# Two quantising pairs on VectorE moved forward in the first stage of a hybrid transformer kernel

## The chip, the cores and the metric

The kernel runs on one core of one Trainium2 chip. The metric is the device time of one execution in microseconds (us). The time before is 2147.03 us, the median of 3 runs (2146.94 to 2148.97).

## The reference, cut to what matters

The program is four layers one after the other on x (2 x 1024 tokens, width 512): a gated linear recurrence, a feed-forward layer, an attention layer, and the feed-forward layer again. The change lies in the first. There, for each block of tokens:

```
proj = layernorm(x) @ w_in.T ; q, k, v, a, g = split(proj, 5)       # 16 heads of 32
q = q * rsqrt(mean(q*q per head) + eps) ; k = tanh(k)
a = clip(sigmoid(a + 2), 0.6, 0.9995) ; u = k * v
prefix = cumprod(a) in chunks of 64 ; acc = cumsum(u / max(prefix, 1e-6))
memory = prefix * (state + acc)
y = sigmoid(g) * (q * memory) + (1 - sigmoid(g)) * v ; x = x + y @ w_out.T
```

The feed-forward layers use ternary weights, which are worked out beside the first layer, since they depend on nothing else:

```
scale = max(mean(|w|) over a group of 64, 1e-8) ; w_hat = clip(round(w / scale), -1, 1) * scale
```

## The kernel before, in words

The first stage fills about the first 406 us. It has 16 steps: four blocks of 512 tokens, and in each four slices c of 128 columns (four heads). Step s projects q, k, v, a and g for its slice. Beside that, each step makes three pieces (128 x 512) of the ternary weights, pieces 3s, 3s+1 and 3s+2. Every engine has its own list of instructions, carried out in the order written; they meet only at semaphores.

TensorE, in step s (L468 to L489): q projection (8 instructions), the group sum of piece 3s (`group`, L440 to L445), k projection, sums of the squares of q (`head_squares`), v projection, group sum 3s+1, in some steps output products or transposes 0 and 1 of a normalised block, a projection, `spread` (transposes of the root that ScalarE made), output products or transposes 2 and 3, g projection, group sum 3s+2. All group sums go to the one PSUM bank 5. So group n waits for `scaled` n, the first of the two quantising instructions of the piece before it.

VectorE, in step s (L754 to L809): `finish(s-1)` (four tensor instructions, L738 to L749: the output of the step before), `normal_rows` where a block is to be normalised (a small reciprocal, and L708 four times), `quantise(3s)` (L727 reads the PSUM bank and frees it, L730 makes the comparison from SBUF), the mean and reciprocal of the head sums (L764, L768), tanh times v (L774), `quantise(3s+1)`, the clip of a (L787, L788), the first scan L791, L793, the product L796 that releases `q_scaled`, the second scan L798, its carry L800, `quantise(3s+2)`, and `normal_stats` in some steps (L691 four times, L694 four times, L696). For a "mid" block `keep_low` (L715) writes the low halves of its transposed rows; for output steps `add_out` (L720) adds to x.

GpSimd (L647 to L664) does four tensor instructions per piece, once its quantising is done. ScalarE (L565 to L604) takes the absolute value and sign of a piece, copies and activates the projections, and makes the root (L586) that `spread` waits for, behind the reciprocal L768. It also loads two activation tables around that root, and copies the transposes (L555).

The tables that say which step does what come out as follows. Norm statistics (`STATS_IN`) stand at the ends of steps 0, 1, 4, 5, 8 and 12. The roots (`ROOT_IN`) come one step later. The rows and transposes (`TURN_IN`) stand in steps 2, 3, 6, 7, 10 and 14. Output products (`OUT_IN`) stand in steps 4, 8 and 12. A step is called free below if it has neither transposes nor output products: 0, 1, 5, 9, 11, 13 and 15.

Of the kernel before, what the change touches and what calls it, by code (L numbers as in the profile page):

```python
# [34 lines left out]
class Steps:  # L35
# [5 lines left out]
    def did(self, ins):  # L41
        ins.then_inc(self.sem, 1)
        self.k += 1
        return ins
# [4 lines left out]
    def settle(self):  # L49

        self.eng.wait_ge(self.sem, self.value())
# [4 lines left out]
NSTEP = NBLK * KT  # L56
NP = 3
# [8 lines left out]
STATS_IN = {at: g for g, (_, _, at) in enumerate(NORMS)}  # L66
ROOT_IN = {at + 1: g for g, (_, _, at) in enumerate(NORMS)}
TURN_IN = {at + 2: g for g, (_, _, at) in enumerate(NORMS)}
OUT_IN = {KT * (i + 1): i for i in range(NBLK - 1)}
# [195 lines left out]
def phase_first(nc, core, x_in, w_inT, w_outT, w_guT, w_pT, wq1, wq2, wk):  # L265

    with ExitStack() as ctx:  # L267
# [47 lines left out]
        def ring(s, j):  # L315
            return bank[(5 * s + j) % 4]
# [14 lines left out]
        def of(g):  # L331
            return NORMS[g][:2] if g < len(NORMS) else ("full", g - len(NORMS))
# [9 lines left out]
        def x_tile(blk, t):  # L342
            return x[:, (blk * TPB + t) * D:(blk * TPB + t + 1) * D]
# [323 lines left out]
        def _(dve):  # L667
# [15 lines left out]
            def normal_stats(g):  # L683
                kind, blk = of(g)
                b = g % 2
                for t in range(TPB):
                    if g == 0:
                        dve.wait_ge(first_loaded[t], 16)
                    elif kind == "in" and t == 0:
                        dve.wait_ge(x_loaded[blk], 16)  # L690
                    did(dve.bn_stats(stats[b][:, 6 * t:6 * t + 6], x_tile(blk, t)))  # L691
                settle()
                for t in range(TPB):
                    did(dve.bn_aggr(mv[b][:, 2 * t:2 * t + 2], stats[b][:, 6 * t:6 * t + 6]))  # L694
                settle()
                did(dve.tensor_scalar(var[b][:, :], mv[b][:, 1:2 * TPB:2], LN_EPS,  # L696
                                      1.0 / (UP * UP) if kind == "mid" else 1.0, ALU.add, ALU.mult))
                settle()
                dve.sem_inc(var_ready, 1)

            def normal_rows(g):
                _, blk = of(g)
                b = g % 2
                dve.wait_ge(root_ready, g + 1)
                did(dve.reciprocal(inv[b][:, :], dev[b][:, :]))
                settle()
                for t in range(TPB):
                    dve.tensor_scalar(row_of(g, t), x_tile(blk, t), mv[b][:, 2 * t:2 * t + 1], inv[b][:, t:t + 1],  # L708
                                      ALU.subtract, ALU.mult).then_inc(rows_ready, 1)

            def keep_low(g, t):
                kind, blk = of(g)
                if kind == "mid":
                    dve.wait_ge(kept, g * TPB + t + 1)
                    dve.tensor_tensor(half(blk, 1, t), turn_bank(g, t), half(blk, 0, t),  # L715
                                      ALU.subtract).then_inc(low_kept, 1)

            def add_out(i, t):
                dve.wait_ge(out_done, i * TPB + t + 1)
                dve.tensor_tensor(x_tile(i, t), x_tile(i, t), out_bank(i, t), ALU.add).then_inc(out_added, 1)  # L720

            def quantise(n):
                b = n % DEPTH
                dve.wait_ge(group_summed, n + 1)
                if n >= DEPTH:
                    dve.wait_ge(made, n - DEPTH + 1)
                dve.tensor_scalar(sc[b], bank[5], 1.0 / GROUP, 1e-8, ALU.mult, ALU.max).then_inc(scaled, 1)  # L727
                dve.wait_ge(scaled, n + 1)

                dve.scalar_tensor_tensor(hit[b], sc[b], 257.0 / 512, wabs[b],  # L730
                                         ALU.mult, ALU.is_lt).then_inc(hits, 1)

            def finish(s):

                i, c = divmod(s, KT)
                vc = v_sb[s % 2]
                dve.wait_ge(q_scaled, s + 1)
                did(dve.tensor_tensor(t1[:, :], prefix[:, :], t2[:, :], ALU.mult))  # L738
                settle()
                did(dve.tensor_tensor(t1[:, :], t1[:, :], vc, ALU.subtract))  # L740
                settle()
                dve.wait_ge(g_kept, s + 1)
                did(dve.tensor_tensor(t1[:, :], t1[:, :], g_sb, ALU.mult))
                settle()
                if i and c == 0:
                    dve.wait_ge(out_done, i * TPB)
                if s < KT:
                    dve.wait_ge(turned, TPB)
                dve.tensor_tensor(yT[:, c * BLK:(c + 1) * BLK], t1[:, :], vc, ALU.add).then_inc(y_ready, 1)  # L749
                dve.wait_ge(y_ready, s + 1)  # L750
# [3 lines left out]
            for s in range(NSTEP):  # L754
                i, c = divmod(s, KT)
                if s:
                    finish(s - 1)
                g = TURN_IN.get(s)
                if g is not None:
                    normal_rows(g)  # L760
                quantise(NP * s)

                dve.wait_ge(sq_summed, s + 1)
                did(dve.tensor_scalar(mean[:, :], bank[4][:, 0:HPQ], 1.0 / HD, RMS_EPS, ALU.mult, ALU.add))  # L764
                settle()
                if s:
                    dve.wait_ge(spread_root, s)
                dve.reciprocal(inv_q[:, :], mean[:, :]).then_inc(inv_ready, 1)  # L768
                if g is not None:
                    dve.wait_ge(turned, g * TPB + 1)  # L770

                dve.wait_ge(tanhed, s + 1)
                dve.wait_ge(v_kept, s + 1)
                did(dve.scalar_tensor_tensor(t1[:, :], ring(s, 1), 1.0 / FLOOR, v_sb[s % 2], ALU.mult, ALU.mult))  # L774
                settle()
                dve.sem_inc(dve_took, 1)
                quantise(NP * s + 1)
                if s in OUT_IN:
                    for t in (0, 1):
                        add_out(OUT_IN[s], t)  # L780
                if g is not None:
                    for t in (0, 1):
                        keep_low(g, t)
                    dve.wait_ge(turned, g * TPB + TPB)

                dve.wait_ge(sigmoided, s + 1)
                did(dve.tensor_scalar(a_first[:, 0:BLK:CH], ring(s, 3)[:, 0:BLK:CH], 0.6, 0.9995, ALU.max, ALU.min))  # L787
                did(dve.tensor_scalar(a_sb[:, :], ring(s, 3), 0.6, 0.9995, ALU.max, ALU.min))  # L788
                settle()
                dve.sem_inc(dve_took, 1)  # L790
                did(dve.tensor_tensor_scan(prefix[:, :], a_sb[:, :], a_first[:, :], 0.0, ALU.mult, ALU.max))  # L791
                settle()
                did(dve.scalar_tensor_tensor(t1[:, :], prefix[:, :], FLOOR, t1[:, :], ALU.min, ALU.mult))  # L793
                settle()
                dve.wait_ge(spread_done, s + 1)
                dve.tensor_tensor(prefix[:, :], bank[4], q_sb[:, :], ALU.mult).then_inc(q_scaled, 1)  # L796
                start = carry[:, c:c + 1] if i % (NBLK // NB) else 0.0
                did(dve.tensor_tensor_scan(t2[:, :], a_sb[:, :], t1[:, :], start, ALU.mult, ALU.add))  # L798
                settle()
                did(dve.tensor_copy(carry[:, c:c + 1], t2[:, BLK - 1:BLK]))  # L800
                if s in OUT_IN:
                    for t in (2, 3):
                        add_out(OUT_IN[s], t)
                if g is not None:
                    for t in (2, 3):
                        keep_low(g, t)
                quantise(NP * s + 2)
                if s in STATS_IN:
                    normal_stats(STATS_IN[s])  # L809
            finish(NSTEP - 1)  # L810

# [1022 lines left out]
```

## Time and profile before

| What | Value |
|---|---|
| median of 3 runs | 2147.03 us |
| the profiled execution's own time | 2146.67 us |
| its span | 2144.8 us |
| mean granted TensorE clock | 0.989 |
| TensorE matmuls busy | 96% of the span |
| VectorE busy | 59% |
| ScalarE busy | 40% |
| GpSimd busy | 41% |

The span goes from the first to the last recorded instruction. The shares are averages over four layers that differ, so a question about the first stage is answered from the rows of its own 406 us. There a step takes 20 to 30 us; a row of the timeline with a bracket says how long its engine stood idle before it and which instruction ended that.

### The profile page before, as it was taken

The numbers are of one execution on the slowest core, as the hardware profiler recorded it, in microseconds if no ns is written. First come the engines' busy times: TensorE is split into PE (matmuls) and PEld (weight loads), VectorE is DVE, ScalarE is ACT, GpSimd is POOL, SyncE is SP. The second block draws the span as 40 slices with busy tenths as digits, with TensorE's granted clock in tenths as the row PEclk, the third lists the DMA queues.
The fourth block names the chain that finished last, engine by engine and source line by source line (L and its number), as shares of the span: only waits on it lengthen the run. The fifth ranks groups of instructions, "written<-read, shape, count | busy, mean of one in ns | idle before, by whom it ended". The sixth has DMA issues, their size and how long they took to land.

```text
span 2144.8 us, 29394 instructions
## 1 busy us (share of the span) xinstructions
PE 2065.8 (96%) x11824; PEld 904.4 (42%) x11824; DVE 1270.5 (59%) x1838; ACT 855.0 (40%) x1304; POOL 888.7 (41%) x457
## 2 busy tenths in 40 slices
PE   7999999999999999999999999999999989999999
PEld 3444444444444444343434344343433333444444
DVE  5868677657755634455555555555556723675634
ACT  4434344334444322344343434343344442443431
POOL 3757585500000001676766565766756681000000
PEclk9999999999999999999999999999999998999999
DMA  7110111300000020000001010000000111000001
GB/s 230 35 34 30 30 35 33 139 0 1 1 1 1 1 61 12 1 16 16 16 11 21 11 21 1 16 16 16 1 11 6 38 52 40 0 1 20 20 1 40
DMA packets 68999, 55.53 MB, mean 26 GB/s; under 512 B 36800, under 2 KB 55232, under 8 KB 68608
## 3 DMA queue, kind: packets, MB, share of 16 engines
q1 hardware_dynamic: 61952, 41.07, 6.6%
q10 hardware_dynamic: 6912, 12.59, 1.9%
q8 instruction: 94, 1.54, 0.3%
q14 instruction: 41, 0.34, 0.1%
HBM read 43.02 MB, written 10.62 MB: 25 GB/s over the span
## 4 chain that ended last, share of the span: by engine, by line
PE 54%; POOL 4%; DVE 3%; ACT 3%; issue 1%; DVEq 0%; POOLq 0%; ACTq 0%
PE psum L116 9%; PE psum L1151 8%; PE psum L1239 8%; PE psum L1269 7%; PE psum L1299 5%; PE psum L140 5%; POOL b_totals L1523 3%; PE psum L1189 3%; PE psum L1245 2%; PE psum L1257 2%; PE psum L1282 2%; PE psum L1197 1%; PE psum L1275 1%; DVE b_maxima L1586 1%; ACT b_probs L1445 1%
## 5 line engine op out<-in xcount | busy, mean ns | idle before, releaser
L1523 POOL TENSOR_TENSOR b_totals<-b_totals,b_probs 128x2048 f32<-128x2048 f32 (+3 forms) x160 | 515.7, 3223 | 324.4 <-ACT b_probs L1445 318.7
L1586 DVE TENSOR_REDUCE b_maxima<-psum 128x2 f32<-128x1024 f32 (+3 forms) x384 | 350.7, 955 | 407.5 <-PE psum L1245 245.2
L1445 ACT ACTIVATE b_probs<-psum 128x1024 f32<-128x1024 f32 (+3 forms) x320 | 228.2, 765 | 269.4 <-PE psum L1282 168.9
L435 PE MATMUL psum<-hT,a_win 128*128 128x512 f32 x640 | 290.8, 597 | 0.8 <-ACT hT L555 0.8
L116 PE MATMUL psum<-hT,b_early 128*128 128x512 f16 x1024 | 229.2, 384 | 5.2 <-DVE b_middle L202 5.2
L116 PE MATMUL psum<-hT,W 128*128 128x512 f16 x1024 | 226.4, 381 | 3.9 <-DVE a_win L202 3.9
L435 PEld LDWEIGHTS psum<-hT,a_win 128*128 128x128 f32 x640 | 119.4, 191 | 129.4 <-issue 128.1
L116 PEld LDWEIGHTS psum<-hT,b_early 128*128 128x128 bf16 x1024 | 100.7, 99 | 132.7 <-issue 12.6
L116 PEld LDWEIGHTS psum<-hT,W 128*128 128x128 bf16 x1024 | 100.5, 98 | 126.4 <-DVE a_win L202 7.6
L1500 POOL MEMSET b_mask<- 128x128 f32 x1 | 0.2, 204 | 356.8 <-POOLq L267 356.8
L1633 DVE RECIPROCAL b_down<-b_down 128x128 f32<-128x128 f32 x128 | 112.0, 918 | 42.7 <-ACT b_down L1423 42.7
L654 POOL TENSOR_TENSOR a_parts<-a_parts 128x512 bf16<-128x512 bf16 x48 | 60.1, 1252 | 132.8 <-DVE a_parts L730 132.8
L1269 PE MATMUL psum<-b_middle 32*128 32x512 f32 (+3 forms) x768 | 105.1, 535 | 5.8 <-ACT b_probs L1445 5.0
L1239 PE MATMUL psum<-b_early 32*128 32x512 f32 (+3 forms) x768 | 105.0, 537 | 5.2 <-ACT b_probs L1445 2.0
L1445 ACT ACTIVATE b_totals<-psum 128x1024 f32<-128x1024 f32 x64 | 62.0, 1021 | 119.4 <-PE psum L1282 64.1
L1239 PE MATMUL psum<-b_middle 32*128 32x512 f32 (+3 forms) x768 | 103.7, 533 | 2.4 <-ACT b_probs L1445 1.5
L202 DVE SCALAR_TENSOR_TENSOR a_win<-psum,a_win 128x512 f32<-128x512 f32 x64 | 44.2, 692 | 99.6 <-ACT a_win L156 98.6
L202 DVE SCALAR_TENSOR_TENSOR b_middle<-psum,lent 128x512 f32<-128x512 f32 x64 | 44.3, 692 | 96.2 <-ACT lent L156 95.7
L1269 PE MATMUL psum<-b_early 32*128 32x512 f32 (+3 forms) x768 | 100.0, 533 | 1.2 <-DVE b_maxima L1586 1.2
L156 ACT ACTIVATE lent<-psum 128x512 f32<-128x512 f32 x64 | 38.2, 597 | 150.9 <-PE psum L116 150.9
L1151 PE MATMUL psum<-hT,b_middle 128*128 128x512 f32 x192 | 97.9, 619 | 0.0
L140 PE MATMUL psum<-b_down,b_probs 128*128 128x512 bf16 x256 | 97.1, 379 | 0.0
(225 smaller groups left out, 3295.7 us busy)
## 6 DMA issues: line engine op xcount, KB each, us to landing
a_parts<-in_w_guT ACTq DMA_DIRECT2D x32, 256.0 KB, 2.8
ternary<-W SPq DMA_DIRECT2D x1, 6144.0 KB, 18.0
a_win<-in_w_inT SPq DMA_DIRECT2D x20, 256.0 KB, 7.3
a_parts<-in_w_pT ACTq DMA_DIRECT2D x16, 256.0 KB, 2.6
b_down<-lam_rows SPq DMA_DIRECT2D x32, 128.0 KB, 2.8
b_early<-ternary SPq DMA_DIRECT2D x8, 512.0 KB, 8.1
out<-x SPq DMA_DIRECT2D x16, 256.0 KB, 2.2
x<-in_x SPq DMA_DIRECT2D x3, 1024.0 KB, 8.0
```

Of the source, the lines that this page charges most:

```text
L116: last = pe.matmul(self.bank[m % 2 * 2 + part], self.gu[:, k * 2 * HID + col:k * 2 * HID + col + P], self.hT[:, at:at + BLK], start=(k + h ...
L140: last = pe.matmul(self.down_bank(j, t), src[:, m * BLK + t * P:m * BLK + (t + 1) * P], self.wd[:, m * D:(m + 1) * D], start=(m + half == ...
L202: dve.scalar_tensor_tensor(self.h[:, m * BLK:(m + 1) * BLK], self.bank[m % 2 * 2 + 1], 1.0 / UP, self.sg[m % 2], ALU.mult, ALU.mult).then_ ...
L435: last = pe.matmul(ring(s, j), win[:, at:at + P], core["hT"][:, (i * KT + k) * BLK:(i * KT + k + 1) * BLK], start=(k == 0), stop=(k == KT ...
L1151: return pe.matmul(to, weights[:, k * P:(k + 1) * P], hT[:, at:at + BLK], start=(k == 0), stop=(k == KT - 1))
L1239: last = pe.matmul(to[j // 2][:, j % 2, 0:width], strip(qT[w][r % 2], j, qt * P, (qt + 1) * P), strip(kT[w][r % 2], j, kc * BLK, hi), star ...
L1269: pe.matmul(to[j // 2][:, j % 2, off:BLK], strip(kT[w][r % 2], j, kt * P, (kt + 1) * P), strip(qT[w][r % 2], j, c * BLK + off, (c + 1) * B ...
L1299: last = pe.matmul(bank[6][HEAD_AT[j] * HD:(HEAD_AT[j] + 1) * HD, off:BLK], v_rows[r // 2 % 2][:, at:at + HD], held(u, s)[:, j, off:BLK], ...
L1445: act.activation(held(u, s)[:, 2 * a:2 * a + 2, off:BLK], pair_banks(("score", u, s, a))[:, :, off:BLK], ACT.Exp, scale=SCALE).then_inc(ex ...
L1523: pool.tensor_tensor(acc, acc, held(u, s)[:, :, off:BLK], ALU.add).then_inc(summed, 1)
L1586: dve.tensor_reduce(maxima[u % 2][:, :].rearrange("p (h q c) -> p h q c", h=HPT, q=QT)[:, 2 * a:2 * a + 2, qt, kc], pair_banks(("row", u, ...
L1633: last = dve.reciprocal(rden[k % 2][:, cols], rden[k % 2][:, cols])
```

## The change: what it does

Only VectorE's order changes. No instruction is added or removed.

```diff
                 if g is not None:
                     normal_rows(g)
-                quantise(NP * s)
+                if s - 1 not in STATS_IN:
+                    quantise(NP * s)
...
                 did(dve.scalar_tensor_tensor(t1[:, :], prefix[:, :], FLOOR, t1[:, :], ALU.min, ALU.mult))
                 settle()
+                busy = s in OUT_IN or g is not None
+                if not busy:
+                    quantise(NP * s + 2)
                 dve.wait_ge(spread_done, s + 1)
                 dve.tensor_tensor(prefix[:, :], bank[4], q_sb[:, :], ALU.mult).then_inc(q_scaled, 1)
...
-                quantise(NP * s + 2)
+                if busy:
+                    quantise(NP * s + 2)
                 if s in STATS_IN:
+                    if s + 1 < NSTEP:
+                        quantise(NP * (s + 1))
                     normal_stats(STATS_IN[s])
```

In the seven free steps `quantise(3s+2)` goes in front of L796 and the second scan. Behind the six steps with statistics, `quantise(3(s+1))` goes from the next step's start (behind `finish` and, in steps 2 and 6, behind the rows) to the end of step s, in front of the statistics. It touches steps 1, 2, 5, 6, 9 and 13.

## Rows read from the trace of the kernel before

**Rows 1.** The page's first part: busy time, share and instructions of each engine.

```profile
PE 2065.8 (96%) x11824; PEld 904.4 (42%) x11824; DVE 1270.5 (59%) x1838; ACT 855.0 (40%) x1304; POOL 888.7 (41%) x457
```

**Rows 2.** TensorE's waits, first 430 us: line, awaited line, us in total, times, longest.

```profile
PE psum L444 <- DVE a_parts L727: 19.1, 15, 3.5
```

**Rows 3.** Timeline, group sums (TensorE L444) of pieces 3, 7, 14 to 19, 30 and 31.

```profile
38.35 0.38 PE L444 MATMUL psum<-a_parts,groupones 128*128 128x512 bf16 x1 [0.89 <-DVE a_parts L727]
...
70.56 0.38 PE L444 MATMUL psum<-a_parts,groupones 128*128 128x512 bf16 x1 [3.50 <-DVE a_parts L727]
...
136.77 0.38 PE L444 MATMUL psum<-a_parts,groupones 128*128 128x512 bf16 x1
140.42 0.38 PE L444 MATMUL psum<-a_parts,groupones 128*128 128x512 bf16 x1
148.40 0.38 PE L444 MATMUL psum<-a_parts,groupones 128*128 128x512 bf16 x1
155.92 0.38 PE L444 MATMUL psum<-a_parts,groupones 128*128 128x512 bf16 x1
160.93 0.38 PE L444 MATMUL psum<-a_parts,groupones 128*128 128x512 bf16 x1 [1.19 <-DVE a_parts L727]
172.06 0.38 PE L444 MATMUL psum<-a_parts,groupones 128*128 128x512 bf16 x1 [3.00 <-DVE a_parts L727]
...
261.54 0.38 PE L444 MATMUL psum<-a_parts,groupones 128*128 128x512 bf16 x1 [1.21 <-DVE a_parts L727]
270.81 0.38 PE L444 MATMUL psum<-a_parts,groupones 128*128 128x512 bf16 x1 [1.14 <-DVE a_parts L727]
```

**Rows 4.** Timeline, VectorE beside GpSimd: `finish` of steps 1 and 4.

```profile
64.17 1.48 POOL L664 TENSOR_TENSOR W<-a_parts 128x512 bf16<-128x512 bf16 x1
64.67 1.52 DVE L740 TENSOR_TENSOR a_t<-a_t,lent 128x512 f32<-128x512 f32 x1
...
142.38 1.15 POOL L664 TENSOR_TENSOR W<-a_parts 128x512 bf16<-128x512 bf16 x1
142.48 1.61 DVE L738 TENSOR_TENSOR a_t<-a_prefix,a_t 128x512 f32<-128x512 f32 x1
144.12 0.69 DVE L740 TENSOR_TENSOR a_t<-a_t,lent 128x512 f32<-128x512 f32 x1
```

**Rows 5.** Timeline, end of step 4 and step 5.

```profile
137.19 0.69 DVE L727 TENSOR_SCALAR a_parts<-psum 128x512 bf16<-128x512 f32 x1 [2.96 <-PE psum L444]
...
149.30 0.69 DVE L774 SCALAR_TENSOR_TENSOR a_t<-psum,lent 128x512 f32<-128x512 f32 x1 [1.21 <-ACT lent L580]
...
150.70 0.61 ACT L586 ACTIVATE a_qq<-a_inv_q 128x512 f32<-128x512 f32 x1
...
153.32 0.17 DVE L787 TENSOR_SCALAR a_a_first<-psum 128x8 f32<-128x8 f32 x1 [1.38 <-ACT psum L594]
```

**Rows 6.** Timeline, second half of step 5.

```profile
156.42 1.46 DVE L793 SCALAR_TENSOR_TENSOR a_t<-a_prefix,a_t 128x512 f32<-128x512 f32 x1
...
160.09 0.69 DVE L727 TENSOR_SCALAR a_parts<-psum 128x512 bf16<-128x512 f32 x1
...
161.59 1.15 POOL L654 TENSOR_TENSOR a_parts<-a_parts 128x512 bf16<-128x512 bf16 x1 [2.69 <-DVE a_parts L730]
```

**Rows 7.** Timeline, step 6, rows, root, transposes and clip.

```profile
169.41 1.00 DVE L708 TENSOR_SCALAR a_t<-x,a_mv,a_inv 128x512 f32<-128x512 f32 x2
...
172.56 0.17 DVE L764 TENSOR_SCALAR a_mean<-psum 128x16 f32<-128x16 f32 x1
...
173.05 0.63 ACT L586 ACTIVATE a_qq<-a_inv_q 128x512 f32<-128x512 f32 x1 [1.76 <-DVE a_inv_q L768]
173.15 3.60 PE L435 MATMUL psum<-hT,a_win 128*128 128x512 f32 x8
...
174.99 1.08 ACT L555 ACTIVATE hT<-psum 128x512 f16<-128x512 f32 x2
...
178.10 0.17 DVE L787 TENSOR_SCALAR a_a_first<-psum 128x8 f32<-128x8 f32 x1 [1.19 <-PE psum L397]
```

**Rows 8.** Stretches: us, busy time by engine, PEclk (granted clock), DMA.

```profile
72.00:74.00 2.00, 2.00 (x3) 0.67 (x2) 1.75 (x3) 1.97 (x4) 1.84 (x3) 0.50 0.00 0
...
170.00:178.00 8.00, 5.93 (x30) 3.98 (x31) 6.59 (x12) 5.49 (x9) 5.04 (x5) 1.00 0.01 2
```

**Rows 9.** Timeline, TensorE's first wait behind step 15.

```profile
406.96 8.38 PE L116 MATMUL psum<-hT,W 128*128 128x512 f16 x32 [3.34 <-DVE a_win L202]
```

## Prediction

> **What bounds the kernel now.** I read the page's engine shares first: TensorE is busy 96% of the span, VectorE 59% [rows 1]. So time is won where TensorE stands idle. The second view is TensorE's waits in the first 430 us, which hold the stage that the change touches. The reader is to see that nearly all of it is one pair of lines: 19.1 us in 15 waits of the group sum L444 for L727, the instruction that frees its PSUM bank [rows 2]. The third view is the timeline at these group sums [rows 3]. Undisturbed, group 3s to group 3s+1 takes 7.98 us (140.42 to 148.40), and the last group of a step to the first of the next 3.65 us (136.77 to 140.42). A wait stretches them: 155.92 to 160.93 is 5.01 us, 1.36 too long, and 160.93 to 172.06 is 11.13, 3.15 too long. The fourth view is VectorE's and GpSimd's timeline beside each other, since the pair that is moved is work of the one and releases the other.
>
> **The change: what could go.** The same measure over the groups that the edits release gives two sums. Third pieces moved ahead of the second scan, in front of groups 3, 6, 18, 30, 36 and 42: 1.05 + 0.30 + 1.36 + 1.37 + 0.34 + 1.37 = 5.79 us. First pieces moved ahead of the statistics, groups 4, 7 and 19: 1.12 + 3.66 + 3.15 = 7.93 us; groups 16, 28 and 40, also released, wait for nothing now. Together 13.7 us, the ceiling. (Groups 3, 7, 18, 19 and 30 stand in rows 3.) The transfers are untouched: SP's and ScalarE's queues keep their order, and ScalarE's loads wait for nothing that moves later.
>
> **Why little of it arrives: VectorE's own chain.** VectorE does as many instructions as before, in another order. Take step 6. It runs without a gap from L787 at 153.32 [rows 5] to L764 at 172.56 and L774 right behind [rows 7]. L764 leads to the reciprocal, ScalarE's root at 173.05, a table load, the copies L555 at 174.99, then VectorE's L715, and only then have transposes 2 and 3 a free bank. The clip L787 at 178.10 had waited only 1.19 us for them. A TensorE that passes group 19 earlier meets this chain again: the first transpose needs the rows L708, ready 0.5 us after 169.41, and these now stand behind 1.4 us more of quantising. With unchanged durations the rows come at 171.3 and 171.8, the a projection starts at 172.6 and not at 173.15, and L764 does not move. The 4.5 us of waits in steps 5 and 6 would give some 0.5 us. Likewise steps 9 to 10 and 13 to 14: VectorE is the later one at group 31 [rows 3], whose L727 has the same work in front of it as before, so the 1.37 us saved at group 30 is waited at group 31.
>
> **What makes it dearer: GpSimd starts in another place.** The clash is seen in [rows 4]. A VectorE instruction with two SBUF inputs takes 0.69 us (L740 at 144.12), but while GpSimd runs it takes 1.5 to 1.6: GpSimd's L664 holds from 142.38 to 143.53, and L738, issued at 142.48, ends at 144.09, 0.69 us after 143.40. L740 at 64.67 and L664 at 64.17 show the alternation: each waits for the other and a pair takes some 1.56 us. So each clash costs VectorE up to 0.85 us. PSUM-fed L727, L774, L796 and the bn_stats do not clash. Now GpSimd gets piece 17 at 161.59 [rows 6] and nothing until L730 of piece 18 near 172.6; in `finish(5)` only L738 clashes. Afterwards piece 17 starts some 1 us earlier and piece 18 follows it without a gap, eight instructions at 1.23 us or more. They cover `finish(5)`.
>
> The Trainium skill, "GPSIMD Engine Reference", section Specifications, says that GpSimd's SBUF interfaces are shared with VectorE and that the contention is with VectorE instructions in a 2-port mode or with two SBUF inputs. Rows 4 agree, with 0.69 against 1.52 us. A reader who counted only the order of semaphores would come out at the 0.5 us gain above; by this rule step 6 comes out later.
>
> **The sum, step by step.** I place each instruction at its row's duration, with the clash rule, and carry the shift.
>
> Steps 4 to 5 (and 8 to 9, 12 to 13). `quantise(15)` must wait for group 15, which ends at 140.80 [rows 3]; `quantise(14)`, whose L727 starts at 137.19, was over at 138.6 [rows 5]. So VectorE stands idle 2.3 us in front of the statistics. Behind it are L696, `finish(4)` and L764, and ScalarE's root waits for them. The statistics end 3.9 us later, with GpSimd's piece 15 beside `finish(4)`: two or three clashes in place of one. L764 goes from 147.6 to about 151.1. L774 had 1.21 us of idle time and L787 1.38, which soak up most of it, but the root goes from 150.70 to 151.6, the spread and the a gate with it: +0.9 us. The three together +2.7. Lower bound 0 (no extra clash: 2.3 us hidden in the 2.6 us of idle time), upper 1.7 each.
>
> Step 6. From L787 at 154.2: L793 ends 158.8, `quantise(17)` 160.3, L796, the scan ends 162.6, `quantise(18)` 164.1, statistics with a late L696 167.6, `finish(5)` with L738, L740 and L743 clashing 173.2, first row 174.0, second 174.4, L764 175.3 in place of 172.56. The a projection starts at 174.9 (173.15 before), ScalarE's root at 175.8, L715 ends 179.6, transposes 180.2 against 178.06. That is +2.1, of which 0.9 is step 5's; own part +1.2. TensorE stands idle from 168.4 to 174.0, 5.2 us and more. In front of group 7 it stood 3.50 us, and the granted clock at 72 to 74 us was 0.50, its 1.2 GHz level, where 3.00 us in front of group 19 left it at 1.00 [rows 3, 8]. At that level eight projection instructions took 5.3 us, not 3.6. So a second such stretch is likely here, partly under the 0.6 us by which the transposes wait for L715: +0.6. Step 6 together +1.8, from -0.5 to +3.
>
> Steps 0 to 2. In step 1 three of four `finish` instructions clash, not one; L764 goes from 47.95 to about 49.9, the root waits for it, spread +0.75. In step 2 L764 comes at about 74.0 in place of 71.05, the second row at 73.2, the a projection at 73.7 against 71.64: +2.0 if the half-clock stretch falls as it does now, +0.6 if it is over before TensorE resumes. I take +1.5; lower bound -1.3 (no extra clash, VectorE's idle time of 0.95 us in step 1 and what follows), upper +3.
>
> Steps 9 to 10 and 13 to 14: GpSimd gets its piece 2.2 us earlier and is done before the rows: -0.2 each. Step 11: -0.3, group 36 no longer waits. Step 15: `quantise(47)` early puts all of GpSimd's piece 47 on `finish(15)`, with L749 at 407.1 against 406.2: +0.9, and TensorE's wait of 3.34 us there grows [rows 9]; bounds 0 and 1.7.
>
> Sum: 1.5 + 2.7 + 1.8 - 0.4 - 0.3 + 0.9 = +6.2 us. Nothing behind the stage takes it up: the next stages begin when this one ends, and TensorE is their bound. The profiled execution took 2146.67 us, its span and 1.9 us around it; 2146.67 + 6.2 = 2152.9. The median lies 0.36 us higher, 2153.2. I forecast 2153.0.
>
> **The rivals.** (1) No clash effect: GpSimd's earlier pieces fit into gaps, VectorE's chain keeps its length. For it: total GpSimd and VectorE work is unchanged, so clashes may only move. Against it: the pieces now lie exactly on `finish`, which has four instructions of two SBUF inputs in a row. Sum of the lower bounds: -1.3 - 0.5 - 0.3 = -2.1, 2144.9 us, no difference that can be told. Chance 0.22.
> (2) Faster: TensorE's waits do end the steps, and freeing the bank early lets it run ahead, with the step's later waits (rows, root) also coming earlier. Its place is groups 4, 7, 19 and the last group of free steps, its price up to 13.7 us, 2133.3 us; it decides once more than 4.3 us of that arrives. For it speaks the wait table, in which L727 is the only large entry; against it the gapless VectorE chain with 1.19 us of room at L787. Half of it would be 2140. Chance 0.10.
> (3) The same mechanism as mine but heavier: a second half-clock stretch at full price and one more clash in each changed step, 8 x 0.85 + 1: some +14 us, 2161. Chance 0.06.
> The forecast has 0.62.
>
> **How the numbers follow.** Differences within 0.2% (4.3 us) can hardly be told from none. Slower by more than that: the forecast's upper part and rival 3, 0.60; within: rival 1 and the forecast's small outcomes, 0.31; faster 0.09. The range reaches from 2145.0, rival 1, to 2158.5.
>
> **What would show it.** Right: the 15 waits for L727 shrink to about 9, those of groups 4, 7 and 19 gone, and new waits of 4 to 6 us of TensorE for L708 in steps 2 and 6. L743 in `finish(5)` at 1.5 us and not 0.69. VectorE idle 2.3 us for group 15. L764 of step 6 later than now by about 2.7 us. Wrong: if L764 in steps 2 and 6 comes no later, or if the a projection of step 6 starts earlier by over 1 us.

## The result and the profile after

The changed kernel takes 2158.78 us, the median of six runs (2154.94 to 2160.71), against 2148.01 for the kernel before (six runs, 2146.94 to 2152.27). The ratio is 1.0046, with a 95% interval of 1.0033 to 1.0058. It is slower by more than the 0.2% that can be told. By the medians that is 10.8 us, by the ratio 9.9. The profiled execution took 2154.94 us, 8.3 us more than that of before, and its page begins:

```profile
span 2153.1 us, 29392 instructions
...
PE 2071.0 (96%) x11824; PEld 906.9 (42%) x11824; DVE 1276.8 (59%) x1838; ACT 855.7 (40%) x1304; POOL 888.5 (41%) x457
```

GpSimd's busy time is that of [rows 1], VectorE's is 6.3 us more with the same 1838 instructions. TensorE's waits in the first 440 us (line, awaited line, us in total, times, longest):

```profile
PE psum L397 <- DVE a_yo L708: 10.3, 1, 10.3
PE psum L397 <- DVE a_t L708: 10.1, 2, 5.9
PE psum L444 <- DVE a_parts L727: 9.4, 6, 2.9
PE psum L116 <- DVE a_win L202: 4.3, 1, 4.3
PE psum L460 <- ACT a_qq L586: 2.0, 1, 2.0
```

Against [rows 2] the waits for L727 have halved. But transposes (L397) now wait 10.1 us for the normalised rows, once 4.2 us in step 2 and once 5.9 in step 6, and the spread (L460) waits 2.0 us for the root. (The first line is the start of the kernel, as before.) The group sums of pieces 14, 17 to 19 and 31, which answer to [rows 3]:

```profile
137.84 0.38 PE L444 MATMUL psum<-a_parts,groupones 128*128 128x512 bf16 x1
...
157.20 0.38 PE L444 MATMUL psum<-a_parts,groupones 128*128 128x512 bf16 x1
160.85 0.38 PE L444 MATMUL psum<-a_parts,groupones 128*128 128x512 bf16 x1
168.82 0.38 PE L444 MATMUL psum<-a_parts,groupones 128*128 128x512 bf16 x1
...
275.14 0.38 PE L444 MATMUL psum<-a_parts,groupones 128*128 128x512 bf16 x1 [2.92 <-DVE a_parts L727]
```

Groups 18 and 19 come at the undisturbed distances, 3.65 and 7.97 us. Group 19 is 3.24 us ahead of the kernel before, and nothing comes of it: TensorE then waits 5.89 us for the rows. Group 31 waits 2.92 us, where it waited 1.14 and group 30 waited 1.21. The timeline of steps 5 and 6 shows why (start, us, engine, line):

```profile
161.41 1.16 POOL L654 TENSOR_TENSOR a_parts<-a_parts 128x512 bf16<-128x512 bf16 x1 [0.63 <-DVE a_parts L730]
...
167.39 1.15 POOL L654 TENSOR_TENSOR a_parts<-a_parts 128x512 bf16<-128x512 bf16 x1
...
168.71 1.60 DVE L738 TENSOR_TENSOR a_t<-a_prefix,a_t 128x512 f32<-128x512 f32 x1
...
170.35 1.52 DVE L740 TENSOR_TENSOR a_t<-a_t,lent 128x512 f32<-128x512 f32 x1
...
171.90 1.52 DVE L743 TENSOR_TENSOR a_t<-a_t,lent 128x512 f32<-128x512 f32 x1
173.46 0.69 DVE L749 TENSOR_TENSOR a_yo<-a_t,lent 128x512 f32<-128x512 f32 x1
...
174.40 1.00 DVE L708 TENSOR_SCALAR a_t<-x,a_mv,a_inv 128x512 f32<-128x512 f32 x2
175.10 1.94 PE L397 MATMUL psum<-ident,a_t 128*128 128x128 f32 x8 [5.89 <-DVE a_t L708]
...
176.23 0.17 DVE L765 TENSOR_SCALAR a_mean<-psum 128x16 f32<-128x16 f32 x1
...
182.49 0.17 DVE L788 TENSOR_SCALAR a_a_first<-psum 128x8 f32<-128x8 f32 x1 [1.91 <-PE psum L397]
```

GpSimd's piece 17 starts at 161.41 and piece 18 follows it at 167.39. Three of the four `finish(5)` instructions clash with it, where one did. Rows, root and clip all move back: the clip from 178.10 [rows 7] to 182.49, while step 5 began only 1.07 us later than before (group 14, 137.84 against 136.77). The same stretch in the table of stretches (PE, PEld, DVE, ACT, POOL busy, granted clock, DMA):

```profile
171.00:179.00 8.00, 3.90 (x12) 2.80 (x13) 7.44 (x13) 2.46 (x5) 1.85 (x3) 0.57 0.01 2
```

The clock of 0.57 is a mean: 6.8 of the eight us are at the 1.2 GHz level, which is called half clock below. Before, 170 to 178 us had 1.00 [rows 8]. Step 1 has a new half-clock stretch too, behind TensorE's wait of 2.0 us for the root. Its g projection of eight instructions, first in the kernel before, then in the changed one:

```profile
51.53 3.60 PE L435 MATMUL psum<-hT,a_win 128*128 128x512 f32 x8
```

```profile
51.73 5.29 PE L435 MATMUL psum<-hT,a_win 128*128 128x512 f32 x8
```

### The profile page after: what moved, and what is told of

Its sections match the earlier page's. It is cut to its first block, busy times and chain, and to the rows that moved or that the text cites. A ratio compares the mean times of both kernels' runs of the same rounds, so it can differ in the third digit from the quotient of the medians.

```text
span 2153.1 us, 29392 instructions
## 1 busy us (share of the span) xinstructions
PE 2071.0 (96%) x11824; PEld 906.9 (42%) x11824; DVE 1276.8 (59%) x1838; ACT 855.7 (40%) x1304; POOL 888.5 (41%) x457
## 4 chain that ended last, share of the span: by engine, by line
PE 53%; POOL 3%; DVE 3%; ACT 3%; issue 1%; DVEq 0%; POOLq 0%; ACTq 0%
PE psum L116 9%; PE psum L1158 8%; PE psum L1246 8%; PE psum L1276 7%; PE psum L1306 5%; PE psum L140 5%; POOL b_totals L1530 3%; PE psum L1196 3%; PE psum L1252 2%; PE psum L1264 2%; PE psum L1289 2%; PE psum L1204 1%; PE psum L1282 1%; DVE b_maxima L1593 1%; ACT b_probs L1452 1%
## 5 line engine op out<-in xcount | busy, mean ns | idle before, releaser
L202 DVE SCALAR_TENSOR_TENSOR a_win<-psum,a_win 128x512 f32<-128x512 f32 x64 | 44.1, 691 | 101.3 <-ACT a_win L156 100.3
L202 DVE SCALAR_TENSOR_TENSOR b_middle<-psum,lent 128x512 f32<-128x512 f32 x64 | 44.2, 691 | 94.8 <-ACT lent L156 94.3
L140 PE MATMUL psum<-W,a_parts 128*128 128x512 bf16 x256 | 97.0, 379 | 0.0
```

What stands on the lines that cost most here:

```text
L140: last = pe.matmul(self.down_bank(j, t), src[:, m * BLK + t * P:m * BLK + (t + 1) * P], self.wd[:, m * D:(m + 1) * D], start=(m + half == ...
L202: dve.scalar_tensor_tensor(self.h[:, m * BLK:(m + 1) * BLK], self.bank[m % 2 * 2 + 1], 1.0 / UP, self.sg[m % 2], ALU.mult, ALU.mult).then_ ...
```

## Where the time went

The shift of the group sums against the kernel before, read at quiet places, in us; behind the stage it is read at L202 of VectorE. The measured column comes from one profiled execution of each kernel:

| Stretch | measured | forecast |
|---|---|---|
| start of the kernel | +0.2 | 0 |
| steps 0 to 3 | +0.9 | +1.5 |
| step 4 to 5 | +0.2 | +0.9 |
| step 6 | +2.4 | +1.8 |
| steps 8 to 10 | +0.5 | +0.7 |
| step 11 | -0.3 | -0.3 |
| steps 12 to 14 | +2.8 | +0.7 |
| step 15 and the end of the stage, to about 520 us | +2.9 | +0.9 |
| everything behind | -1.3 | 0 |
| sum | +8.3 | +6.2 |

The last two rows rest on the same instruction in both kernels, first before, then changed (9.58 us later):

```profile
518.69 0.69 DVE L202 SCALAR_TENSOR_TENSOR a_win<-psum,a_win 128x512 f32<-128x512 f32 x1
```

```profile
528.27 0.69 DVE L202 SCALAR_TENSOR_TENSOR a_win<-psum,a_win 128x512 f32<-128x512 f32 x1
```

So the stage costs 9.4 us in the traces, without the start. The later stages, which the change does not touch, give 1.3 us back; the execution of the kernel before had 39 us of half clock there, that of the changed kernel 34.

## The experiments

All ran on one core as before. Ratios are against the kernel before, run beside them. In the traces a step's shift is counted from the clip of step 0, since the start differs by up to 2.6 us between executions.

**1. Third pieces alone.** The edit: `quantise(NP * s)` back in its old place.

```diff
-                if s - 1 not in STATS_IN:
-                    quantise(NP * s)
+                quantise(NP * s)
...
-                    if s + 1 < NSTEP:
-                        quantise(NP * (s + 1))
```

> Only the third pieces go in front of the second scan in the seven free steps; the first pieces stay. Clash theory (VectorE's chain has the same work, GpSimd's earlier start only moves which instructions clash): waits for L727 at groups 30 and 42 are gone and those at groups 31 and 43 grow by the same 1.4 us, group 36 gains 0.3 us, the whole within -1 to +3 us of before. Rival (TensorE's waits end the steps): faster by 5 to 6 us. Clock theory (the excess over the instruction sum is half-clock stretches of TensorE behind long waits): the wait of about 2.9 us at groups 31 and 43 may bring one such stretch, +1.7 us each, whatever the ports do.

Measured: 2148.51 us, ratio 1.0005 (0.9995 to 1.0015). By the median, the 5.8 us of waits that this edit frees bring nothing. In its one trace the clip of step 15 does come 4.7 us earlier, counted from step 0. There 1.7 us is the half-clock stretch of step 2, which this execution doesn't have, and 0.8, 0.4 and 0.9 us are gained in steps 1, 2 to 3 and 6; steps 10, 12 and 14 add 0.2 to 0.3 each. But run 6 has a second trace with the same order up to step 14, and there the clip of step 15 comes no earlier at all (0.1 us later). That execution has 10.2 us of half clock in steps 2 and 6, where the trace of run 1 has none. So some 3 us of the waits arrive, and in the other trace half-clock stretches took them back. The waits at groups 31 and 43 grow to 2.3 us. At the end TensorE's first wait behind the stage has the 4.26 us of the changed kernel, not the 3.34 of [rows 9]: step 15's part of the loss is in this edit.

**2. First pieces alone.** The edit: every step counts as busy for the third piece.

```diff
-                busy = s in OUT_IN or g is not None
+                busy = True
```

> Only the first pieces go in front of the statistics; the third pieces stay. Clash theory: most of the loss is here, +4 to +8 us against before, with TensorE waiting 4 to 6 us for L708 in steps 2 and 6. Rival (the two edits cost only together, since the second makes GpSimd's two pieces run without a gap): within 2 us of before. Rival (TensorE's waits end the steps): faster by 7 to 8 us.

Measured: 2152.88 us, ratio 1.0018 (1.0009 to 1.0028). It is slower by 3.5 us, just under the 4 to 8 that were expected, and 0.05% and 0.18% do not add up to 0.46%. The trace is from another execution of the same kernel, of which this was expected:

> The same kernel as the run with the first pieces alone, for its trace. Clash theory: in step 6 two or three instructions of finish(5) at 1.5 us (piece 17 starts later than with both edits, piece 18 right behind it), TensorE waits about 3.8 us for L708, the clip of step 6 1 to 2 us later than before; in steps 5, 9 and 13 VectorE waits 2.3 us for the group sum and the clip loses 0.2 to 0.3 us each. Rival (the loss is in the waits for groups 15, 27 and 39): 1 us or more at each of these.

```profile
PE psum L444 <- DVE a_parts L727: 13.4, 11, 1.8
...
PE psum L397 <- DVE a_t L708: 9.5, 2, 4.8
```

TensorE's waits for the rows are here already: 4.8 us at most, more than the 3.8 expected. All four instructions of `finish(5)` take 1.5 us, where two or three were expected and the changed kernel has three. So the rival's reason, that only both edits together put GpSimd's pieces on `finish`, is refuted. From the clip of step 4 to that of step 6 it loses 4.2 us, where 1 to 2 were expected. In steps 5, 9 and 13 VectorE waits 2.2 us for the group sum and the clip comes 0.85 us later each time, not 0.2 to 0.3. So the group-sum wait has a price, but the 1 us and more of the rival is not reached.

Why the two edits cost more together may be seen in the half-clock time of the first 450 us: 23.9 us in the changed kernel, 6.8 in each of the traces of the kernel before, of run 1 and of run 2. Half of TensorE's busy time in these stretches, an estimate of what they cost from these four traces, is 9.4 us against 3.0, 2.9 and 3.3. The 6 us of difference are as large as what is missing in the sum (0.23%, 4.9 us). With one execution of each kernel this is not shown for the medians.

**3. GpSimd's work cut short.** Three of its four instructions per piece work on 8 columns, in the kernel before and in the changed one. The weights are not rounded and scaled then.

```diff
-                p.did(pool.tensor_tensor(sc[b], sc[b], wabs[b], ALU.subtract))
+                p.did(pool.tensor_tensor(sc[b][:, 0:8], sc[b][:, 0:8], wabs[b][:, 0:8], ALU.subtract))
...
-                p.did(pool.tensor_tensor(hit[b], hit[b], sc[b], ALU.mult))
+                p.did(pool.tensor_tensor(hit[b][:, 0:8], hit[b][:, 0:8], sc[b][:, 0:8], ALU.mult))
```

> The kernel before, with GpSimd's first three instructions per piece cut from 512 to 8 columns (so the ternary weights are not rounded and scaled as they should be); the fourth stays whole. It is the base for the next run. Clash theory: most of VectorE's 1.5 us instructions of finish, the products and the scans fall to 0.7 to 1.2, VectorE's chain in steps 2, 3, 6, 7, 10 and 14 is shorter, TensorE's waits for L727 fall from 19 to under 12 us, the time by 5 to 12 us. If GpSimd's work does not hold VectorE: no change.

> The changed kernel with the same cut of GpSimd's work. Against the kernel before with that cut: by the clash theory the loss is gone, -3 to +1 us (ports no longer matter, only the order of VectorE's instructions, whose rows in steps 2 and 6 come later by 1.4 us but whose roots come as before). If the loss is the order itself (rows behind the quantising, the wait for group 15), it stays: +5 us or more.

Measured: 2121.59 us for the kernel before with the cut, ratio 0.9870 (0.9856 to 0.9884), and 2123.25 for the changed one, 0.9879 (0.9865 to 0.9893). The cut gives 28 us, much more than the 5 to 12 expected; TensorE's waits for L727 are gone but for 1.9 us in two, where under 12 us was expected. And the loss of 10.8 us shrinks to 1.7 by the medians of four runs each, and the two intervals overlap. In the traces the changed kernel gains 0.3 us of the stage from step 0 to step 15, where it lost 6.5 with the whole work, and neither trace has a half-clock stretch in the stage. So without the clash neither the longer chain nor the lower clock is there, and the new order by itself costs nothing that can be told. The same VectorE line with GpSimd whole and cut (us in total, mean ns), first the kernel before and then its cut version:

```profile
L740 DVE TENSOR_TENSOR a_t<-a_t,lent 128x512 f32<-128x512 f32 x16 | 20.2, 1265 | 0.6
L749 DVE TENSOR_TENSOR a_yo<-a_t,lent 128x512 f32<-128x512 f32 x16 | 19.4, 1215 | 0.6
L743 DVE TENSOR_TENSOR a_t<-a_t,lent 128x512 f32<-128x512 f32 x16 | 19.4, 1213 | 0.5
L738 DVE TENSOR_TENSOR a_t<-a_prefix,a_t 128x512 f32<-128x512 f32 x16 | 16.5, 1031 | 0.9
```

```profile
L749 DVE TENSOR_TENSOR a_yo<-a_t,lent 128x512 f32<-128x512 f32 x16 | 11.1, 692 | 0.5
L743 DVE TENSOR_TENSOR a_t<-a_t,lent 128x512 f32<-128x512 f32 x16 | 11.1, 692 | 0.5
L740 DVE TENSOR_TENSOR a_t<-a_t,lent 128x512 f32<-128x512 f32 x16 | 11.1, 692 | 0.6
L738 DVE TENSOR_TENSOR a_t<-a_prefix,a_t 128x512 f32<-128x512 f32 x16 | 11.0, 687 | 0.9
```

The 64 `finish` instructions take 75.5 us with GpSimd whole and 44.3 with it cut. In the changed kernel they take more:

```profile
L740 DVE TENSOR_TENSOR a_t<-a_t,lent 128x512 f32<-128x512 f32 x16 | 24.4, 1525 | 0.6
L743 DVE TENSOR_TENSOR a_t<-a_t,lent 128x512 f32<-128x512 f32 x16 | 21.9, 1369 | 0.6
...
L738 DVE TENSOR_TENSOR a_t<-a_prefix,a_t 128x512 f32<-128x512 f32 x16 | 19.3, 1206 | 0.9
L749 DVE TENSOR_TENSOR a_yo<-a_t,lent 128x512 f32<-128x512 f32 x16 | 17.8, 1110 | 0.6
```

Their sum is 83.4 us, 7.9 more. It lies in `finish` of steps 0 and 5 (1.6 us each, three of four slowed and not one) and of steps 1, 4, 8, 11, 12 and 15 (0.7 to 0.8 each); the others are as before to 0.2 us.

**4. GpSimd held until `finish` is over.** VectorE's order is that of the changed kernel.

```diff
                 pool.wait_ge(w_sign, n + 1)
+                if j == 0 and s - 1 in STATS_IN:
+                    pool.wait_ge(y_ready, s)
```

> The changed kernel, VectorE's order untouched, but GpSimd may start the moved first piece (3s in steps 1, 2, 5, 6, 9 and 13) only when finish(s-1) is over, so that these instructions have the port for themselves. Clash theory: finish(5) back to 0.7 us per instruction behind L738 or L740, TensorE's waits for L708 shorter by 1.5 to 2.5 us each, the time 4 to 9 us under the changed kernel, 2150 to 2155. If the order itself (rows behind the quantising, wait for group 15) makes the loss: within 1.5 us of the changed kernel, or later by the held pieces.

Measured: 2155.81 us, ratio 1.0036 (1.0023 to 1.0049), 3 us under the changed kernel and just outside what the clash theory gave. Its trace has 27.3 us of half clock in the first 450 us, the most of all, so one execution does not say how much of the rest is clock. `finish(5)` is at 0.69 us four times, as expected. TensorE's wait for the rows fell to 3.4 us in step 6, but in step 2 it grew from 4.2 to 4.4, where both were expected to fall by 1.5 us or more. What was gained there was lost at the next instructions:

```profile
170.47 0.69 DVE L751 TENSOR_TENSOR a_yo<-a_t,lent 128x512 f32<-128x512 f32 x1
...
171.40 2.65 DVE L710 TENSOR_SCALAR a_t<-x,a_mv,a_inv 128x512 f32<-128x512 f32 x2
173.97 1.37 DVE L710 TENSOR_SCALAR a_prefix<-x,a_mv,a_inv 128x512 f32<-128x512 f32 x1
175.27 1.37 DVE L710 TENSOR_SCALAR a_a<-x,a_mv,a_inv 128x512 f32<-128x512 f32 x1
```

The rows (L708 in the unheld kernels, L710 here) have one SBUF input each and clash all the same, 1.3 us in place of 0.5 [rows 7].

**5. GpSimd held until the rows are written.** In steps 2 and 6 it waits for the rows, in the others for `finish`.

```diff
+                if j == 0 and s - 1 in STATS_IN:
+                    if s in TURN_IN:
+                        pool.wait_ge(rows_ready, (TURN_IN[s] + 1) * TPB)
+                    else:
+                        pool.wait_ge(y_ready, s)
```

> As the held run, but in steps 2 and 6 GpSimd's moved piece waits until the four rows L708 are written, since in the held run these took 1.3 us each in place of 0.5. Clash theory: rows back to 2 us for four, TensorE's wait for L708 in steps 2 and 6 down by 0.5 to 1.5 us each, the time 2 to 4 us under the held run, 2152 to 2154. If the order of VectorE's instructions makes the remaining loss: as the held run.

Measured: 2148.58 us (12 runs, 2144.83 to 2150.23), ratio 0.9997 (0.9989 to 1.0006). This wait on GpSimd takes the whole loss away, 10 us, 7 of them against run 4. That is more than the 2 to 4 expected there. VectorE's order, its wait for group 15 and the rows behind `quantise` are all still in it. The hold takes away more than the change had added: `finish` of steps 0, 4, 5, 8 and 12 runs without a clash, where the kernel before had one in each. So it alone does not say that the order is free; run 3 does. Half clock in the first 450 us of its trace is 13.7 us. Step 6 with this wait:

```profile
166.87 0.69 DVE L743 TENSOR_TENSOR a_t<-a_prefix,a_t 128x512 f32<-128x512 f32 x1
...
169.05 0.69 DVE L754 TENSOR_TENSOR a_yo<-a_t,lent 128x512 f32<-128x512 f32 x1
...
170.91 0.54 DVE L713 TENSOR_SCALAR a_prefix<-x,a_mv,a_inv 128x512 f32<-128x512 f32 x1
171.36 0.54 DVE L713 TENSOR_SCALAR a_a<-x,a_mv,a_inv 128x512 f32<-128x512 f32 x1
171.82 0.17 DVE L770 TENSOR_SCALAR a_mean<-psum 128x16 f32<-128x16 f32 x1
...
176.96 0.17 DVE L793 TENSOR_SCALAR a_a_first<-psum 128x8 f32<-128x8 f32 x1 [0.75 <-PE psum L397]
```

From `finish`'s end to the mean it is 2.1 us, where run 4 needed 5.4. TensorE's two waits for the rows are 3.8 and 2.6 us (4.4 and 3.4 in run 4, 4.2 and 5.9 in the changed kernel).

**6. The last step's third piece.** `busy` also holds for step 15, once on top of run 1 and once on top of run 5.

```diff
+                busy = s in OUT_IN or g is not None or s == NSTEP - 1
```

> Third pieces in front of the second scan in the free steps except 15, first pieces as before. Clash theory: the 0.9 us that the clash on finish(15) cost (TensorE's wait for L202 was 4.26 us in place of 3.34) is back, and the half-clock stretch behind it is shorter: 1 to 3 us under the run with all seven free steps, 1 to 4 us under before. If the ordering in step 15 does not matter: as that run, 2148.5.

> As the run before it, and step 15's third piece stays behind the scan, as in the kernel before. Clash theory: 0.9 us less in front of L202 and a shorter half-clock stretch there, 1 to 3 us under the run before it, 2150 to 2153; by none of the theories does it beat the kernel before by more than its scatter. If step 15 does not matter: as the run before it.

Measured: 2149.52 us, ratio 1.0004 (0.9993 to 1.0015), on top of run 1, which is a miss: 1 to 3 us less were expected. Its runs scatter from 2142.2 to 2152.9, so an effect of 0.9 us can't be told. On top of run 5 it is 2146.64, ratio 0.9991 (0.9982 to 0.9999), 2 us under run 5, as expected, though the intervals overlap, and barely under before, where no gain was expected. In both traces the wait for L202 is back at 3.3 us. The half-clock stretch behind it is shorter in the second only (3.4 us, 6.8 in the first).

**7. TensorE kept busy while it waits.** Products that are thrown away, written to the bank of the next transposes. First in the changed kernel:

```diff
+                if s in (2, 6):
+                    free(("norm", TURN_IN[s], 0))
+                    for _ in range(4 if s == 2 else 6):
+                        pe.matmul(turn_bank(TURN_IN[s], 0).rearrange("p k t -> p (k t)"), win[:, 0:P],
+                                  core["hT"][:, 0:BLK], start=True, stop=True)
```

> The changed kernel, with extra projection-sized products (4 in step 2, 6 in step 6, each 0.86 us) that TensorE throws away, where it now stands idle 4.2 and 5.9 us for the rows. Clock theory (the part of the loss beyond the instruction sum is half-clock stretches behind those waits): no half-clock stretch at steps 2 and 6, the clip of step 6 some 1 to 2 us earlier than in the changed kernel, the time 2 to 4 us under the changed kernel's 2158.8, about 2155. If the clock had no part: as the changed kernel, or up to 1 us later where the filling overruns the rows.

Measured: 2155.79 us, ratio 1.0035 (1.0023 to 1.0047), 3.0 us under the changed kernel by the medians, though the intervals overlap. The half-clock stretches of steps 2 and 6 are gone and the clip of step 6 comes 1.6 us earlier, as expected. Stretches of 3.4 us stand in steps 1, 10 and 14, that of step 10 being new, and the long one at the end. By the clip of step 15 this trace is 0.5 us behind that of the changed kernel: what step 6 gained is lost again, in steps 7 and 10. So the 3 us rest on the medians alone. Then in the kernel before (three products in front of the second group sum) and on top of the better kernel of run 6, both also at the end of the stage:

```diff
+                if m == 2:
+                    pe.wait_ge(q_scaled, NSTEP)
+                    for _ in range(12):
+                        pe.matmul(bank[4], W[:, 0:P], h16[:, 0:BLK], start=True, stop=True)
```

> The kernel before, VectorE and GpSimd untouched, with products that TensorE throws away in its longest waits: three of 0.86 us in front of the second group sum in steps 2 and 6, and twelve of 0.22 us in front of L116 at the end of the stage. Clock theory: the half-clock stretches at these places go, 1 to 4 us less than before, 2145 to 2148. If half-clock stretches cost nothing that counts: no change, or 0.5 us more where the filling overruns.

> The held run with step 15 as before, plus the same filling (three products in step 2, two in step 6, twelve at the end of the stage). If port and clock are separate costs that add up: 1 to 3 us under that run's 2146.6, 2143.5 to 2146, and below before by more than its scatter. If the clock has no part: 2146.6.

Measured: the kernel before with the filling takes 2142.23 us (11 runs, 2141.84 to 2146.34), ratio 0.9976 (0.9966 to 0.9986). It is the fastest kernel of the study that does the whole work. The gain is 6.6 us by the medians and 5.2 by the ratio (3.0 to 7.3), above the 1 to 4 that were expected. Its stretches at step 2 and at the end of the stage, which answer to [rows 8] and [rows 9]:

```profile
70.00:75.50 5.50, 4.37 (x18) 2.60 (x19) 4.22 (x8) 3.00 (x4) 3.75 (x3) 1.00 0.00 0
...
405.00:425.00 20.00, 19.84 (x77) 8.95 (x78) 5.58 (x10) 3.98 (x7) 0.39 (x1) 1.00 0.94 355
```

The clock is 1.00 in both; in the kernel before it was 0.69 and 0.91 in the same stretches. The 32 products at the stage's end, first in the changed kernel (two of 32 records are missing), then in this one:

```profile
414.56 9.61 PE L116 MATMUL psum<-hT,W 128*128 128x512 f16 x30 [4.26 <-DVE a_win L202]
```

```profile
405.15 7.08 PE L116 MATMUL psum<-hT,W 128*128 128x512 f16 x32 [0.74 <-DVE a_win L202]
```

In the kernel before they took 8.38 us [rows 9]. Not all of the gain is explained by this. Two instructions of VectorE behind the stage, first in the filled kernel; the first of them started at 518.69 in the kernel before (see above), and the second as the last row here says:

```profile
515.84 0.69 DVE L202 SCALAR_TENSOR_TENSOR a_win<-psum,a_win 128x512 f32<-128x512 f32 x1
...
1853.41 0.69 DVE L202 SCALAR_TENSOR_TENSOR b_middle<-psum,lent 128x512 f32<-128x512 f32 x1
```

```profile
1858.12 0.69 DVE L202 SCALAR_TENSOR_TENSOR b_middle<-psum,lent 128x512 f32<-128x512 f32 x1
```

So the filled kernel is 2.9 us ahead just behind the stage and 4.7 us ahead near the end of the program. The difference arises behind 1778 us, in a stage that the filling does not touch. There, from 1760 us on, the execution of the kernel before has 27.3 us of half clock and this one 20.5. Whether the filling has a part in that is not shown.

On top of the held kernel the filling gave nothing: 2147.64 us, ratio 0.9993 (0.9984 to 1.0002), a miss against 2143.5 to 2146. Its profiled execution has a span of 2140.0 us, as good as the 2140.1 of the filled kernel before. But 11 of its 12 runs are slower than that, at mean clocks of 0.989 to 0.990, where 8 of 11 of the other are at 0.992 or 0.993. The slower runs have the lower mean clock, but the one profiled execution has no half-clock stretch in the stage, so no trace says where the time is lost. That stays open.

## Why the prediction was right, step by step

The forecast was 2153.0 us, +6.2 in its own terms; the profiled execution came out at +8.3 and the median at +10.8. That is 0.3 us above the range's upper end of 2158.5. As ratios, forecast, measured and end of the range are 1.0028, 1.0046 and 1.0053. The upper bounds of the terms add up to +12.1, or 2159.1, so the range was also set a little too narrow for its own terms. The direction and the mechanism hold, but by its number the median is nearer to rival 3 (2161) than to the forecast.

That the traces' +8.3 lies near +6.2 is in part luck, since two errors cancel: the wait for group 15 was priced too high by about 1.3 us, the half-clock stretches by several us too low. And one view was read too broadly: the 19.1 us of [rows 2] were not nearly all of TensorE's waits in the first 430 us, which were 33.4 us, with 10.2 at the kernel's start and 3.3 behind step 15.

- **What could go.** Groups 3, 4, 6, 7, 18, 19, 30, 36 and 42 no longer wait for L727: right. Six waits are left; nine were forecast. At group 31 the saved 1.37 us came back, as forecast (2.92 us).
- **VectorE's chain.** Right in steps 10 and 14, where run 1 gains 0.2 to 0.3 us out of 1.4. In steps 1 to 3 and 6 run 1's trace has 2.1 us of gain that I had not given the third pieces; the trace of the same order in run 6 has none. At the median it is 0.9 us, within the interval.
- **The clash.** Right, and the cause of the loss: cutting GpSimd's work (run 3) or changing only its place in time (run 5) takes the loss away. `finish(5)` came out as forecast to the instruction, three at 1.5 to 1.6 us and L749 at 0.69. The mean of step 6 was forecast at 175.3, with step 5 starting as before; with that start 1.07 us later it came at 176.23, within 0.2 us.
- **The wait for group 15.** VectorE's idle time was forecast at 2.3 us three times. VectorE's waits for the group sums in the changed kernel:

```profile
DVE a_parts L727 <- PE psum L444: 22.8, 7, 7.2
```

It was 16.0 us in four waits before, so three more waits of 2.2 us: right. Its price was mis-sized. TensorE lost 0.2 us in step 5 and not 0.9 (and the same in steps 9 and 13), since the spread had 0.7 us of room behind the root that I had not given it (the root ends at 153.22, the spread starts at 153.27). The clip did come 0.84 us later, and steps 10 and 14 paid 0.4 us each for it. Together 1.4 us, where the forecast had 2.7.
- **The half-clock stretches.** This term was the one sized most wrongly, and the likely reason why the median lies at the range's edge. I gave it 0.6 us in step 6 and part of the 1.5 us of steps 0 to 2. The trace has 61 us of half clock over the whole kernel against 49 before, and 23.9 against 6.8 in the first 450 us. By the estimate under run 2 that is 6.4 us of lost time, some of it already counted in the steps above. Step 1 has one that I had not forecast (its g projection takes 5.29 us in place of 3.60). In step 6 it is 6.8 us long. In step 14 a wait of 2.92 us brought another: groups 43 to 44 take 10.96 us where they took 9.27, 1.7 us. At the stage's end it is 6.8 us and not 3.4. Run 7 shows in the kernel before that such time is real: filling the waits gives 6.6 us by the medians, 2.9 of them seen in the trace by the end of the stage. In the changed kernel it gives 3.0 us, with overlapping intervals.
- **Step 15.** TensorE's wait for L202 grew from 3.34 to 4.26 us: +0.9, as forecast.
- **Rival 1, no clash effect:** refuted by runs 3 and 5. **Rival 2, TensorE's waits end the steps:** refuted at its full price by run 1; some 3 us of the 5.8 arrive in its trace, and none in that of run 6. **Rival 3, heavier:** the further half-clock stretches in it came true; `finish(5)` has no further clash.

Not settled: the other five runs of the changed kernel took 3.3 to 5.8 us more than the profiled one, at almost the same mean clock (0.985 or 0.986 against 0.986). More half clock can explain only part of that: 0.001 of mean clock is at most 2.2 us, and the run of 2160.43 us has the 0.986 of the profiled one, which took 2154.94. What the rest is, no trace shows.

## What to carry to other kernels

Before an instruction is moved forward on VectorE, look at what it releases on GpSimd and what VectorE does in that time. Here the moved pairs cost nothing that can be told by themselves, and GpSimd's eight instructions in a row behind them made three of the four in `finish(5)` twice as long. A table of waits says where an engine stands, not what the time is worth: 13.7 us of TensorE's waits could be freed, and next to none of it arrived, because VectorE's chain was no shorter. Longer waits also brought half-clock stretches, so a small loss on VectorE grew on TensorE. Work that is thrown away in waits that must be can be worth more than a better order: in the kernel before, with waits of 3.5, 3.0 and 3.3 us filled, it gave 6.6 us, and the order at best 2. It did not add up with the held order, so it has to be measured in each kernel.

## What the runs showed of the hardware

- A VectorE instruction with one SBUF input and fp32 data (the rows, 0.54 us each) is slowed by GpSimd as one with two inputs is, to 1.37 us (run 4). The Trainium skill, "GPSIMD Engine Reference", section Specifications, names two kinds of VectorE instruction that contend with GpSimd, those with two SBUF inputs and those in a 2-port mode. The trace agrees that more than the first kind does; that the rows run in a 2-port mode is not shown by any run here. I had counted only the first kind.
- Waits of TensorE of 2.9 us at groups 31 and 43 had no half-clock stretch at the one and one at the other, in the same execution. In the filled run of the changed kernel, with the same two waits, both had one. In the trace of run 1 waits of 4.0 and 3.4 us in steps 2 and 6 had none. So one profile is no measure of them: the runs of one kernel lie 2 to 11 us apart.
- GpSimd's three full-width instructions per piece cost the whole kernel 28 us (run 3), though no other engine's wait in this stage is put down to it. GpSimd is busy 41% of the span, and 64% of the first 406 us.
